# Half-row loads, a ring of three and earlier late attentions in a graph-attention kernel

## The reference

```python
feats    = (X @ W).reshape(-1, H, D)                       # X: 8192 x 64
a_self   = einsum('nhd,hd->nh', feats, att_self)
a_neigh  = einsum('nhd,hd->nh', feats, att_neigh)
scores   = leaky_relu(a_self.T[:, :, None] + a_neigh.T[:, None, :], 0.2)
scores   = scores + (-1e10 * (1.0 - A))[None, :, :]        # A: 8192 x 8192, fp32, 0 or 1
attn     = softmax(scores, axis=-1)
out      = relu(einsum('hij,jhd->ihd', attn, feats) + bias)
result   = layernorm(X + out)
```

## Time and profile before

| | us |
|---|---|
| median of three runs (lowest to highest) | 844.21 (843.2 to 846.03) |
| the profiled execution, its own time | 844.56 |
| span of the profiled execution, first to last instruction | 842.7 |
| PE busy / DVE busy / POOL busy / ACT busy | 600.1 / 587.8 / 502.0 / 78.2 |
| last matmul of the last block ends | 748.4 |

### The profile page before, as it was taken

How to read it: one execution, slowest core, us unless ns; L and a number is a source line. 1 busy time by engine, 2 the same in 40 slices (tenths; PEclk the granted TensorE clock), 3 DMA queues, 4 the chain that set the end, 5 groups by cost and what they waited for, 6 DMA issues and landing times.

```text
span 842.7 us, 8722 instructions
## 1 busy us (share of the span) xinstructions
PE 600.1 (71%) x2132; PEld 289.6 (34%) x2133; DVE 587.8 (70%) x1683; ACT 78.2 (9%) x355; POOL 502.0 (60%) x464
## 2 busy tenths in 40 slices
PE   2766665588669797868888786976769685835564
PEld 1621111146314352433424251533335141504343
DVE  5567994641796878676666675677668977847885
ACT  1200000210010101000001000011020110102010
POOL 4100977777607777777777777766464757636400
PEclk9885555558979988886868695989799696958787
DMA  7999999999999999999999999999999999931100
GB/s 284 363 413 389 408 391 345 329 359 398 399 419 404 398 399 397 401 396 399 398 399 399 398 398 398 397 400 396 373 369 408 399 406 397 403 136 27 37 1 25
DMA packets 76230, 291.79 MB, mean 346 GB/s; under 512 B 31318, under 2 KB 39307, under 8 KB 43408
## 3 DMA queue, kind: packets, MB, share of 16 engines
q1 hardware_dynamic: 56784, 275.44, 83.4%
q0 software_dynamic: 14208, 10.46, 4.3%
q10 hardware_dynamic: 5184, 5.31, 1.9%
HBM read 294.39 MB, written 4.75 MB: 355 GB/s over the span
## 4 chain that ended last, share of the span: by engine, by line
DMA 52%; PE 27%; DVE 13%; issue 5%; SPq 1%; ACT 1%; DVEq 0%; ACTq 0%
DMA adj_sb<-in_adj_dram 51%; PE xt_ps L676 13%; PE codes L648 11%; DVE spare L926 2%; DVE head_mask L792 1%; PE ft_ps L633 1%; PE xt_ps L678 1%; PE ft_ps L717 1%; SPq L402 1%; DVE top L912 1%; DMA base<-in_L_gnn_att_self_dram 1%; DVE z L903 1%; DVE z L911 1%; DVE z L915 0%; DVE z L906 0%
## 5 line engine op out<-in xcount | busy, mean ns | idle before, releaser
L444 POOL DMA_INDIRECT near<-node_table,idx x444 | 489.6, 1103 | 278.6 <-issue 192.9
L648 PE MATMUL codes<-adj_sb,weights 128*128 128x512 bf16 x1024 | 349.5, 482 | 165.1 <-DMA adj_sb<-in_adj_dram 164.8
L648 PEld LDWEIGHTS codes<-adj_sb,weights 128*128 128x128 bf16 x1024 | 100.6, 109 | 393.7 <-issue 339.2
L676 PE MATMUL xt_ps<-spare,ident 128*128 128x360 f32 (+4 forms) x734 | 195.4, 416 | 29.6 <-DVE spare L926 29.6
L676 PEld LDWEIGHTS xt_ps<-spare,ident 128*128 128x128 f32 x734 | 135.5, 198 | 81.5 <-issue 41.8
L816 DVE MAX8 val<-codes 128x8 f32<-128x128 f32 x192 | 42.7, 284 | 140.7 <-PE codes L648 134.0
L926 DVE TENSOR_TENSOR spare<-near,spare 128x704 f32<-128x704 f32 (+12 forms) x64 | 101.1, 1641 | 9.1 <-ACT spare L571 9.1
L821 DVE MAX8 val<-codes 128x8 f32<-128x64 f32 (+2 forms) x156 | 19.6, 198 | 42.8 <-PE codes L648 42.0
L571 ACT ACTIVATE spare<-z 128x736 f32<-128x736 f32 (+10 forms) x16 | 14.9, 933 | 215.4 <-DVEq L918 215.4
L641 PE MATMUL codes<-place,weights 128*128 128x512 bf16 x64 | 31.3, 490 | 0.0
L872 DVE MAX8 key<-left 128x8 f32<-128x168 f32 (+2 forms) x79 | 28.7, 363 | 2.7
(11 more groups left out here) (156 smaller groups left out, 483.6 us busy)
## 6 DMA issues: line engine op xcount, KB each, us to landing
adj_sb<-in_adj_dram SPq DMA_DIRECT2D x256, 1024.0 KB, 16.7
near<-node_table,idx POOLq DMA_INDIRECT x444, 5.8
node_table<-spare ACTq DMA_DIRECT2D x4, 648.0 KB, 7.9
spare<-in_x_dram SPq DMA_DIRECT2D x4, 512.0 KB, 7.7
self_sb<-node_table ACTq DMA_DIRECT2D x16, 121.5 KB, 7.6
x_sb<-in_x_dram SPq DMA_DIRECT2D x4, 384.0 KB, 18.1
out_dram<-x_sb SPq DMA_DIRECT2D x1, 768.0 KB, 12.6
self_sb<-node_table ACTq DMA_DIRECT2D x16, 40.5 KB, 10.1
```

The costliest lines, as they stand in the source:

```text
L444: pool.indirect_dma_start(out=near[:, near_at(t) + k, :], out_offset=None, in_=table[:, :], in_offset=bass.IndirectOffsetOnAxis(ap=idx[t % ...
L648: last = pe.matmul(codes[i][:, :], weights[:, kk, :], adj_bf[q][:, k * GC:(k + 1) * GC, 1], start=False, stop=(kk == BITS - 1))
L676: last = pe.matmul(to[:, a:b, :], ident[:, :], slot_rows(t, s, a, b), start=(s == 0), stop=(s == W - 1))
```

## The change

Three edits. First, `near` is cleared by DVE as its first instruction, without a wait, and no longer by POOL. Second, `ATTEND` from tile 6 on: the attentions of tiles 6 to 15 begin one to three steps earlier, tiles 5 to 10 three steps apart; `sum_at` and `finish_at` follow from the list. Third, each block is loaded as two halves of [128 x 4096], 2 MB each, into three half slots (48 KB of a partition in place of 56). PE waits once for a half and packs two quarters from it; SP waits until both quarters of the half three before are packed.

```diff
-    ATTEND = [16, 20, 24, 28, 32, 36, 40, 44, 47, 50, 53, 57, 60, 64, 67, 70]
+    ATTEND = [16, 20, 24, 28, 32, 36, 39, 42, 45, 48, 51, 55, 58, 61, 64, 67]
...
-    ADJ_RING = 7
+    HALVES = 2
+    ADJ_RING = 3
...
-        adj_sb = sb("adj_sb", [P, ADJ_RING, N // QUARTERS], fp32)
+        adj_sb = sb("adj_sb", [P, ADJ_RING, N // HALVES], fp32)
...
-                for h in range(QUARTERS):
-                    m = QUARTERS * n + h
+                for h in range(HALVES):
+                    m = HALVES * n + h
...
-                        sp.wait_ge(quarters_packed, m - ADJ_RING + 1)
+                        sp.wait_ge(quarters_packed, QUARTERS // HALVES * (m - ADJ_RING + 1))
...
-            pool.wait_ge(weights_ready, 1)
-            pool.memset(near[:, :, :], 0.0).then_inc(near_zeroed, 1)
...
                 for h in range(QUARTERS):
-                    m = QUARTERS * n + h
-                    q = m % ADJ_RING
-                    wait_apart(pe, adj_loaded[q], 16 * (m // ADJ_RING + 1))
+                    half, part = divmod(QUARTERS * n + h, QUARTERS // HALVES)
+                    q = half % ADJ_RING
+                    if part == 0:
+                        wait_apart(pe, adj_loaded[q], 16 * (half // ADJ_RING + 1))
...
+            dve.memset(near[:, :, :], 0.0).then_inc(near_zeroed, 1)
             dve.wait_ge(params_loaded, 64)
```

More of the change, by code:

```diff
@@ L332, in of_sbuf @@
             return a[:, blocks, :] if blocks.start < NH else a[:, blocks, :].rearrange("p (t j) c -> p t (j c)", j=REST)
-        adj_heads = adj[0:NH * P, :].rearrange("(b p) (h c) -> p b h c", p=P, h=QUARTERS)
-        adj_rest = adj[NH * P:N, :].rearrange("(t p j) (h c) -> p t j h c", p=P, j=REST, h=QUARTERS)
+        adj_heads = adj[0:NH * P, :].rearrange("(b p) (h c) -> p b h c", p=P, h=HALVES)
+        adj_rest = adj[NH * P:N, :].rearrange("(t p j) (h c) -> p t j h c", p=P, j=REST, h=HALVES)
         adj_bf = [adj_sb[:, q, :].bitcast(bf16).rearrange("p (c two) -> p c two", two=2) for q in range(ADJ_RING)]
@@ L642, in pack @@
                 for h in range(QUARTERS):
-                    m = QUARTERS * n + h
-                    q = m % ADJ_RING
-                    wait_apart(pe, adj_loaded[q], 16 * (m // ADJ_RING + 1))
+                    half, part = divmod(QUARTERS * n + h, QUARTERS // HALVES)
+                    q = half % ADJ_RING
+                    if part == 0:
+                        wait_apart(pe, adj_loaded[q], 16 * (half // ADJ_RING + 1))
                     for k in range(BITS // QUARTERS):
                         kk = h * BITS // QUARTERS + k
-                        last = pe.matmul(codes[i][:, :], weights[:, kk, :], adj_bf[q][:, k * GC:(k + 1) * GC, 1],
+                        last = pe.matmul(codes[i][:, :], weights[:, kk, :], adj_bf[q][:, (part * BITS // QUARTERS + k) * GC:(part * BITS // QUARTERS + k + 1) * GC, 1],
                                          start=False, stop=(kk == BITS - 1))
```

## The result

The changed kernel takes 848.08 us (median of five runs, 846.88 to 848.35) against 844.21 before: 1.0041 times as long, with a 95% interval of 1.0024 to 1.0059. It is 0.4% slower. The forecast was 837.6 us and faster; its range of 831 to 853 holds the time, its sign was wrong.

The account below looks back on a forecast made before the run. Loading bounds the kernel until the last block is packed, then a tail: 748.4 - 0.5 + 8.2 - 2 + 2 = 756.1, plus 80.0 is 836.1; with 1.86 outside 838.0, less 0.35 gives 837.6 us, range 831 to 853.

Parts of the forecast that it names:

- What bounds the kernel: Whole span: loading keeps the DMA engines busy until the last block is packed, then a 94.3 us tail of DVE, ACT, PE.
- E: Time at which the last block is packed: 748.4 us before the change, forecast 756.1 after it.
- Clearing: At the start: DVE clears in 11.7 us, reaches its later steps about 4 us earlier; last block packed 0.5 us earlier.
- The allowance of 9.9 us: Loading with three halves: longest time from landing to packed without stopping loading, 2 x 5.68 less 1.5 us overhead.
- Pieces shrink by about 0.5 from tile to tile: tile 2 is at 10.0, the rest inside.: Blocks with a sum: tile 0 over by 4.0 us, tile 1 by 1.5, tile 2 by 0.1, later tiles stop nothing.
- the allowance of 15.5 us: Loading with seven quarters: longest time from a quarter's landing to packed without stopping loading, 17.0 less 1.5 us.
- The clash at block 42: Tile 6's sum at block 42 waits for DVE's late `weigh`; its halves run over by 0.6 and 2.0, together 2.6 us.
- The long rows: All loading: rows twice as long save half the fixed cost per row, taken as 2 us, bounds 0 and 13.
- the prediction's third rival: All loading: sums overlap landings without stops, 8.2 us less, 829.4 us; cites 2.0 us per DMA plus bytes; chance 0.14.
- The +2: Block 62: tile 12's sum, some 8 us of PE, makes the last block packed 2 us later.
- The tail: After the last block is packed: 10.0 + 29.6 + 3 + 7.45 + 30.0 = 80.0 us, where it was 94.3.
- The first rival: Every block with a sum: engines running ahead cut the allowance to 7.9 us, 26 us of stops, 855.4 us; chance 0.22.

Follow-up runs that it names:

- the second experiment: Only the clearing of `near` moved from POOL to DVE, in the kernel before the change: 845.21 us beside 845.01, ratio 0.9999.

## Why the prediction was wrong

**What bounds the kernel** was right: loading until the last block, then a tail. The difference lies in E, 8.3 us over the forecast, and in the branch at the end, which no term of the forecast covers. E over 762 was one of the forecast's own signs of being wrong.

**Clearing.** It took 9.24 us, as POOL's own MEMSET in the earlier trace rows and not as the operation with inputs in the earlier trace rows; the forecast took 11.7 and had 9.28 as its bound. It begins at 3.11 us, where the forecast had it begin at the start. The two misses nearly cancel, by luck: DVE's next step begins at 12.34 (forecast 11.8). DVE comes to `above` at 19.69, 3.7 us earlier (forecast 4.0), and `head_mask` takes 0.20 us. POOL's preparations beside the clearing are not held up: the last of them starts at 3.71 us in both kernels. By the second experiment it is worth nothing (forecast 0.5 us); loading is saturated then.

**The allowance of 9.9 us** for holding a half was made of two overheads, and one of them was right, SP's issue to data: a half of block 51 is released at 638.88, and the load engines are at

```profile
638.00:639.00 1.00, 1.00 (x7) 0.66 (x6) 0.00 (x0) 0.00 (x0) 0.00 (x0) 1.00 0.10 19
639.00:640.00 1.00, 1.00 (x11) 1.00 (x10) 0.97 (x5) 0.00 (x0) 0.00 (x0) 1.00 0.60 131
```

again about 1 us. From the data's end to PE's start 0.5 was estimated, with 1 as the upper bound. The packet records give 1.2 us at block 51 (622.1 to 623.35) and 1.0 to 2.1 us for the first halves of the table's twelve blocks, over the bound in ten of them. The data's end is counted here over all 16 load engines together; the last of them signals its landing at 623.21, and PE starts 0.14 us later, as it does in eleven of the twelve. The table's held begins at the data's end, so its limit is 2 x 5.68 - 1.0 = 10.4 us, and the stops do begin between 9.2 and 10.8. In the forecast's own count, from PE's side, the allowance was 8.3 to 9.4 us, not 9.9.

**The step that failed** is the sentence "Pieces shrink by about 0.5 from tile to tile: tile 2 is at 10.0, the rest inside." It ran a series on from the pieces of blocks 20 and 24, which had run with PE's clock up. With PE kept busy the first pieces do shrink (5.72, 4.88, then 4.28 and 3.67, block 42 apart), and from block 32 on a half is held for 10.6 us at most, again but for block 42. In the changed kernel the first piece took 5.0 to 6.8 us in nine of the eleven blocks after block 20, because PE came to it from idling and ran at half clock for part of it. The trace of the kernel before had both levels, here at the start of the first pieces of blocks 24 and 32 (PEclk is the third column from the end):

```profile
302.00:304.00 2.00, 2.00 (x9) 1.33 (x8) 1.75 (x9) 0.00 (x0) 1.42 (x2) 1.00 1.03 402
392.00:394.00 2.00, 2.00 (x6) 1.25 (x4) 1.86 (x9) 0.00 (x0) 1.44 (x2) 0.55 1.02 406
```

The forecast took 1.88 us for the first quarter of a half that PE had waited for and 0.90 for the ones behind a piece, which is about what PE takes at the two levels, but it took every piece at the full one. The half clock did not come with the halves alone. The list with seven quarters, at block 51:

```profile
608.91 1.86 PE L646 MATMUL codes<-adj_sb,weights 128*128 128x512 bf16 x4 [0.57 <-DMA adj_sb<-in_adj_dram]
610.57 1.40 PE L674 MATMUL xt_ps<-spare,ident 128*128 128x360 f32 x2
...
610.00:612.00 2.00, 2.00 (x5) 1.22 (x4) 1.88 (x8) 0.00 (x0) 1.70 (x2) 0.50 1.02 409
```

There this first piece takes 5.05 us (5.84 with halves), and over the eleven blocks after block 20 the mean is 4.9 us with quarters, 5.4 with halves and 4.2 with PE kept busy. With quarters the allowance of 15.5 us takes it in and the traffic stays at 398 GB/s; three halves have no room for it. The short estimate from the data's end to PE's start, 0.5 to 1.6 us of the same sums, made the room smaller still. Block 20 lost 4 us as forecast, block 24 some 3.5 (forecast 1.5), and each of seven later sums 0.4 to 1.8 us where the forecast had 0.1 for all.

**The clash at block 42** was seen, and undersized: 7 us for 2.6.

```profile
514.16 1.86 PE L648 MATMUL codes<-adj_sb,weights 128*128 128x512 bf16 x4 [2.43 <-DMA adj_sb<-in_adj_dram]
520.81 1.54 PE L676 MATMUL xt_ps<-spare,ident 128*128 128x360 f32 x2 [4.78 <-DVE spare L927]
```

`weigh` ends at 520.5, 7.6 us behind the half's data (forecast 34 - 28.4 = 5.6), and the first piece, begun after a wait of 4.78 us, takes 6.80 us in place of 4.0, at half clock again. PE kept busy ahead of the block helps little there (6.30 us): this wait is inside it.

**The long rows** were put at 2 us (bounds 0 and 13). By traffic without stops (402 to 398) they give 1%, 5 us from 200 to 700 and some 7 over all loading. That compares a kernel without most of its sums to one with them. Ahead of the first sum, two kernels with all their sums show the same (long rows, then 8 KB rows, both with the pieces behind two quarters):

```profile
200.00:250.00 50.00, 32.50 (x150) 16.16 (x155) 35.69 (x91) 4.51 (x23) 22.09 (x22) 0.88 1.01 410
200.00:250.00 50.00, 37.10 (x156) 16.19 (x158) 35.45 (x91) 4.52 (x23) 21.13 (x22) 0.78 1.02 405
```

With the long rows the last block of these two is packed 5.4 us earlier. The changed kernel reached only 406 GB/s in the same stretch. The Trainium skill (DMA: Bandwidth & Descriptors, "Rules for kernel authors") asks for at least 1 MiB a transfer and to coalesce small ones; both kernels are on the right side of that rule. Twice the size gained some 5 us by itself, and three slots of it still came out 12 us of loading behind six slots of the single size. The fit of 2.0 us a DMA that the prediction's third rival takes from the Trainium skill was measured there on DMAs that GpSimd issues, while SP issues these loads; the prediction rightly gave it no weight.

**The account.** 748.4 + 26 of stops - 7 of long rows = 767, measured 764.4; the forecast had 8.2, -2 and +2. The +2, for tile 12's sum in block 62, did not show at the end: PE waits 0.30 us there for the last half.

**The tail**: `idx` at E + 10.4 (forecast 10.0), the gathers end 29.1 us later (29.6), the scores begin 1.5 us behind (landing 3), 7.4 to the weighing, 33.2 to the end (30.0, said to be unchanged; the long branch is 3.2 of it). 81.6 for 80.0; DVE waits for POOL as said. Without the branch it would be 78.4: the landing's 1.5 us and the branch's 3.2 are misses that partly cancel.

**The first rival** came close in time (855.4) and in place (every block with a sum). It had the 26 us of stops. Its mechanism is borne out in part: it said that engines which run ahead of the last one shorten the allowance by 2 us, and the late last engine took 0.5 to 1.6 us more of it than forecast (above). The rest is what it did not have, halves held longer by first pieces at half clock. How much the clock makes is shown for the changed kernel alone: keeping PE busy took 7.1 us off the loading and left 17 of the 26 us of stops ((402 - 388) / 402 x 500), at block 20, 24, 28 and 42 for the most part. What the added matmuls cost PE in those 17, and what the short estimate of PE's start did, was not measured apart.

## What to carry to other kernels

A ring of a few large slots is priced by how long one slot is held in its worst visit, landing and release both; what stands between the two belongs behind the release (16 us here, for three lines). Take the durations of work behind a wait at the clock that the wait leaves: a series read while the engine was busy does not hold there, and a ring with less room shows it. When a change has several parts, the one that looks like a free saving (here some 5 us of long rows) can hide a gain of 13 us made by the others. Before a difference of a few us is put down to the change, look where in the span it lies: 3 us here are one branch at the end.

## What the runs showed of the hardware

PE's granted clock was at 0.50 after a wait of 3.50 us and stayed there through the 5.7 us of matmuls without a pause that followed (623.35 to about 629); the second piece then took 3.67 us for the work that had taken 5.84. The Trainium skill (TensorE: Matmul & The Clock Gate, "HAM oscillation — how this bites in real kernels") tells of this pattern, a short stretch of matmuls behind each wait for a load that starts cold every time; the rows agree for nine of the table's twelve blocks. Blocks 20, 32 and 48 began their first piece with the clock up, behind waits of 1.1 to 2.0 us, and ran it through at that level. Here the cost was not PE's own time but the loads that its late release held back.

Clearing 11016 elements took DVE 9.24 us and POOL 9.28, so a MEMSET of this size is no faster on DVE, though an operation of 8192 elements with two inputs takes 8.67 us there.

One branch in PE's instruction queue took 3.3 to 3.8 us in five kernels and 0.37 in the others, at the same place of the program. No run shows why.
